# A gated linear attention kernel: scores and state updates as 64x64 products on quarters of the TensorE array

## The reference

```python
x = L0_attn_hidden_states                                 # (16, 512, 128)
q = relu(heads(norm(x) @ Wq)); k = relu(heads(norm(x) @ Wk)); v = heads(norm(x) @ Wv)
g = log_sigmoid(norm(x) @ Wg1 @ Wg2 + bg2) / 16           # one gate for each key feature
S_t = exp(g_t)[:, None] * S_{t-1} + k_t (outer) v_t       # a 64x64 state for each kv head
o_t = (q_t / 8) @ S_t
o = g_norm_weight * o * rsqrt(mean(o*o) + eps)            # per head
x = x + norm(o @ Wo)
x = x + norm(experts(norm(x)))                            # top 2 of 8, silu(x gate) * (x up), down
```

## Time and profile before

| what | value |
|---|---|
| time, median of 3 runs | 1351.63 us (1347.49 to 1352.96) |
| the profiled execution, its time | 1356.56 us |
| its span, first to last instruction | 1354.7 us |
| PE busy | 1251.3 us, 92% |
| DVE / ACT / POOL busy | 58% / 50% / 41% |
| one sequence in the middle of the loop | 55.2 us, PE busy 51.7 us |
| query phase of that sequence | 13.2 us, PE busy 10.6 us |
| expert tiles and sums | from about 925 us to the end |

### The profile page before, as it was taken

One profiled execution on the slowest core, in us unless ns is written; L12 is line 12 of the kernel. 1 busy time (PEld: TensorE's weight loads), 2 busy tenths in 40 slices (PEclk: granted clock), 3 DMA queues, 4 the chain that ended last, 5 costly groups with the idle time before them and its releaser, 6 DMA issues.

```text
span 1354.7 us, 27688 instructions
## 1 busy us (share of the span) xinstructions
PE 1251.3 (92%) x8062; PEld 1045.2 (77%) x8062; DVE 791.5 (58%) x2380; ACT 676.3 (50%) x1717; POOL 550.3 (41%) x671
## 2 busy tenths in 40 slices
PE   8999999989999899998998989956999999999895
PEld 5877868779687686786877868755989998998772
DVE  5676766667766676676766776662333333333327
ACT  4655547456464464654746547332444444444336
POOL 2244443544534435344363443332333333333326
PEclk9999999999998999999999999987999999999998
DMA  6000010100100001001010010132411111111335
GB/s 255 9 25 19 21 31 13 34 27 12 39 12 27 31 8 39 14 25 31 8 39 16 23 31 5 31 127 81 126 49 47 49 47 47 49 49 43 111 135 209
DMA packets 59674, 67.47 MB, mean 50 GB/s; under 512 B 6896, under 2 KB 49664, under 8 KB 59264
## 3 DMA queue, kind: packets, MB, share of 16 engines
q1 hardware_dynamic: 48720, 41.10, 9.6%
q0 software_dynamic: 8448, 17.45, 3.9%
q10 hardware_dynamic: 2480, 8.61, 2.0%
HBM read 37.98 MB, written 29.15 MB: 50 GB/s over the span
## 4 chain that ended last, share of the span: by engine, by line
PE 75%; DVE 10%; issue 6%; DMA 3%; ACT 3%; another core or an unknown queue 1%; POOL 1%; DVEq 1%; ACTq 0%; POOLq 0%; SPq 0%
PE pO L756 8%; PE pA L579 8%; PE pO L595 8%; PE pO L597 6%; PE pA L561 5%; PE pW L624 4%; PE pA L747 4%; PE pA L748 4%; PE pJ L747 4%; PE pJ L748 4%; PE pO L569 4%; PE pJ L561 3%; PE pT L607 3%; DVE kT L1103 2%; PE pJ L624 2%
## 5 line engine op out<-in xcount | busy, mean ns | idle before, releaser
L1591 POOL DMA_INDIRECT expert_out<-y,tail x136 | 130.5, 960 | 262.5 <-ACT y L1024 235.3
L595 PE MATMUL pO<-vJ,aT 128*128 128x128 f32 x1024 | 194.0, 279 | 0.0
L873 ACT ACTIVATE sq<-pO 128x512 f32<-128x512 f32 x128 | 75.9, 593 | 213.3 <-PE pO L595 170.4
L597 PE MATMUL pO<-S_mid,qT 128*128 128x128 f32 x896 | 173.2, 275 | 0.0
L595 PEld LDWEIGHTS pO<-vJ,aT 128*128 128x128 f32 x1024 | 153.8, 192 | 14.7 <-issue 13.2
L569 PEld LDWEIGHTS pO<-vJ,kJ 128*128 128x128 f32 x448 | 68.4, 200 | 102.6 <-issue 52.4
L1151 DVE TENSOR_REDUCE ss<-sq 128x8 f32<-128x512 f32 x128 | 86.6, 676 | 100.7 <-ACT sq L873 100.7
L1523 POOL DMA_INDIRECT expert_rows<-x1n,rowi x120 | 117.5, 979 | 65.0 <-issue 43.6
L597 PEld LDWEIGHTS pO<-S_mid,qT 128*128 128x128 f32 x896 | 136.0, 192 | 0.0
L579 PE MATMUL pA<-qT,kT 128*128 128x256 f32 x512 | 132.8, 383 | 0.0
L756 PE MATMUL pO<-wdown_sb,vJ 128*128 128x128 f32 x1088 | 132.7, 275 | 0.0
(11 more groups left out here) (239 smaller groups left out, 2602.3 us busy)
## 6 DMA issues: line engine op xcount, KB each, us to landing
xt<-expert_rows SPq DMA_DIRECT2D x69, 130.0 KB
xa<-x SPq DMA_DIRECT2D x16, 256.0 KB, 2.7
xr<-x SPq DMA_DIRECT2D x16, 256.0 KB, 2.8
after_attention<-x SPq DMA_DIRECT2D x16, 256.0 KB
arena<-after_attention ACTq DMA_DIRECT2D x8, 512.0 KB
expert_rows<-zeros SPq DMA_DIRECT2D x8, 390.0 KB
expert_out<-y,tail POOLq DMA_INDIRECT x136
wgate_sb<-wgate SPq DMA_DIRECT2D x1, 2048.0 KB, 9.9
```

Source lines behind the costliest of these rows:

```text
L595: last = mm(o, aT[:, c % 2, p, h * P:(h + 1) * P], vJ[:, c, p, :], start=True, stop=(c == 0))
L597: last = mm(o, qT[:, p, c, 2 * h:2 * h + 2, :].rearrange("p r c -> p (r c)"), S_mid[:, c, p, :], start=False, stop=True)
L1591: g.indirect_dma_start(out=ys_dram, in_=y[:, k, :], in_offset=None, out_offset=bass.IndirectOffsetOnAxis(ap=tail[:, k, 1:2].bitcast(U32), ...
```

## The change

Keys are stored compactly: `kT` holds 64 columns for each pair and chunk and has no zeros, `kJ` one 128x128 block a chunk. Scores are computed by 64x64 products: four for a chunk, one for each head, on the four quarters of the array (rows by head `h`, output partitions by pair `p`). They are issued for two chunks at a time, behind one semaphore increment. State updates are four 64x64 products of 64 columns a chunk, all 28 of them behind the second query. `S_raw` is 64 wide; `mids` on POOL spreads it back over two blocks with a mask of the halves (`own_step`). `outputs` does its four products of masked scores first and then the four with the state. DVE computes `kT` with two instructions on 128 partitions, the keys are seven transposes, and ACT copies them with two instructions.

```diff
-            def key_transposes(j, groups):
-                for p in range(PAIRS):
-                    pe.wait_ge(k_ready, j * 4 + 2 * p + 2)
...
-                        for c in range(2 * g, min(2 * g + 2, NC - 1)):
-                            last = tr(key_bank[g][:, ((c % 2) * 2 + p) * P:((c % 2) * 2 + p + 1) * P],
-                                      kT[:, p, c, :], ident)
+            def key_transposes(j):
+                pe.wait_ge(k_ready, j * 2 + 2)
+                for c in range(NC - 1):
+                    last = tr(key_bank[c // 4][:, c % 4 * P:(c % 4 + 1) * P],
+                              kT[:, c, :, :].rearrange("p a c -> p (a c)"), ident)
...
+            def project_queries(j, turns=range(PAIRS * R)):
+                for b in turns:
+                    if b < 2:
+                        pe.wait_ge(v_ready, j * 8 + 4 * b + 4)
+                    elif b < 4:
+                        pe.wait_ge(k_ready, j * 2 + b - 1)
+                    else:
+                        pe.wait_ge(q_ready, j * 8 + b - 3)
+                    mm(four[b % 4][:], wq_sb[:, b // R, b % R, :], xnT[:],
+                       start=True, stop=True).then_inc(q_psum, 1)
+                    if b == 1:
+                        state_updates(j)
+
+            def state_updates(j):
+                pe.wait_ge(kJ_ready, j * 2 + 2)
+                settle(pe)
+                for c in range(NC - 1):
+                    for p in range(PAIRS):
+                        for h in range(2):
+                            rows = slice(p * C, p * C + C)
+                            last = mm(pR[h * D:(h + 1) * D, p, c * D:(c + 1) * D], kJ[rows, c, h * D:(h + 1) * D],
+                                      vJ[rows, c, h, p * D:(p + 1) * D], start=True, stop=True)
+                last.then_inc(upd_psum, 1)
...
                 if c >= 2:
-                    pe.wait_ge(a_ready, i * NC + c - 1)
-                for p in range(PAIRS):
-                    if c < 2:
-
-                        pe.wait_ge(q_ready, i * 8 + (8 if p == 1 else 5 + c))
-                    last = mm(pA[c % 2][:, p, :], kT[:, p, c, :],
-                              qT[:, p, c, :, :].rearrange("p r c -> p (r c)"), start=True, stop=True)
+                    pe.wait_ge(a_ready, i * NC + c)
+                else:
+                    pe.wait_ge(q_ready, i * 8 + 8)
+                settle(pe)
+                for n in (c, c + 1):
+                    for p in range(PAIRS):
+                        for h in range(2):
+                            rows = slice(h * D, h * D + D)
+                            last = mm(pS[p * C:(p + 1) * C, h, n % 2 * R * C:(n % 2 + 1) * R * C], kT[rows, n, p, :],
+                                      qT[rows, p, n, :, :].rearrange("p r c -> p (r c)"), start=True, stop=True)
                 last.then_inc(a_psum, 1)
...
-                    if c + 2 < NC:
+                    if c % 2 == 0 and c + 2 < NC:
                         scores(i, c + 2)
...
-                    for half in range(2):
-                        rows = slice(half * D, half * D + D)
-                        v.scalar_tensor_tensor(
-                            out=kT[rows, p, :, half * C:half * C + C],
+                    v.scalar_tensor_tensor(
+                        out=kT[:, :, p, :], in0=pJ[p][:].rearrange("p (n c) -> p n c", c=C), scalar=0.0,
...
-                            scalar=step[:, p, c - 1:c], in1=pO[c % 2][:, p, :], op0=ALU.mult, op1=ALU.add)
+                            scalar=step[:, p, c - 1:c], in1=came[:, p, :], op0=ALU.mult, op1=ALU.add)
...
+                g.tensor_tensor(own_step[:, :, 0:NC - 1, :], wide(step[:, :, 0:NC - 1].unsqueeze(3), P, PAIRS, NC - 1, 2),
+                                wide(own_half.unsqueeze(1).unsqueeze(1), P, PAIRS, NC - 1, 2), ALU.mult)\
+                    .then_inc(own_ready, 1)
...
-                    g.tensor_tensor(S_mid[:, c + 1, :, :], S_raw[:, c % 2, :, :],
-                                    wide(step[:, :, c:c + 1], P, PAIRS, P), ALU.mult).then_inc(mid_ready, 1)
+                    g.tensor_tensor(S_mid[:, c + 1, :, :].rearrange("p a (h v) -> p a h v", h=2),
+                                    wide(S_raw[:, c % 2, :, :].unsqueeze(2), P, PAIRS, 2, D),
+                                    wide(own_step[:, :, c, :].unsqueeze(3), P, PAIRS, 2, D), ALU.mult)\
+                        .then_inc(mid_ready, 1)
```

More of the change, by code:

```diff
@@ L61 @@
 C_RB = C_RW + E
-C_LEAST = C_RB + E
+C_HALF = C_RB + E
+C_LEAST = C_HALF + 2
 C_END = C_LEAST + E
@@ L534, in project_values @@
                     last.then_inc(v_psum, 1)
-            def key_transposes(j, groups):
-                for p in range(PAIRS):
-                    pe.wait_ge(k_ready, j * 4 + 2 * p + 2)
-                    for g in groups:
-                        if p == 0 and g < 3 and not at_start(j):
-                            pe.wait_ge(*((on_ready, j * NC), (on_ready, j * NC), (ot_ready, j * NC))[g])
-                        for c in range(2 * g, min(2 * g + 2, NC - 1)):
-                            last = tr(key_bank[g][:, ((c % 2) * 2 + p) * P:((c % 2) * 2 + p + 1) * P],
-                                      kT[:, p, c, :], ident)
-                        if p == PAIRS - 1:
-                            last.then_inc(kJ_psum, 1)
@@ L591, in outputs @@
                     pe.wait_ge(mid_ready, i * (NC - 1) + c)
+                o = pO[c % 2][:].rearrange("t (p g) (h v) -> t g h p v", p=PAIRS, h=2)
+                for h in range(2):
+                    for g in range(2):
+                        last = mm(o[:, g, h, :, :], aT[:, c % 2, h, g * P:(g + 1) * P], vJ[:, c, h, :],
+                                  start=(h == 0 and g == 0), stop=(c == 0), skip_group_check=True)
                 for p in range(PAIRS):
-                    for h in range(2):
-                        o = pO[c % 2][:, 2 * p + h, :]
-                        last = mm(o, aT[:, c % 2, p, h * P:(h + 1) * P], vJ[:, c, p, :], start=True, stop=(c == 0))
+                    for g in range(2):
                         if c > 0:
-                            last = mm(o, qT[:, p, c, 2 * h:2 * h + 2, :].rearrange("p r c -> p (r c)"),
-                                      S_mid[:, c, p, :], start=False, stop=True)
+                            last = mm(pO[c % 2][:, 2 * p + g, :],
+                                      qT[:, p, c, 2 * g:2 * g + 2, :].rearrange("p r c -> p (r c)"),
+                                      S_mid[:, c, p, :], start=False, stop=True, skip_group_check=True)
                 last.then_inc(o_psum, 1)
@@ L630, in chunks @@
                 scores(i, 0)
-                scores(i, 1)
                 for c in range(NC):
@@ L706, in turn @@
                 project_values(i + 1)
-                key_transposes(i + 1, range(NC // 2))
+                key_transposes(i + 1)
                 merge_heads(i, NT - 1, True)
-                project_queries_and_states(i + 1)
+                project_queries(i + 1)
             turn(0, False)
@@ L857, in values @@
                         came = slice(odd * C, odd * C + C)
[L858 to L861 removed]
+                        for p in range(PAIRS):
+                            goes = slice(p * C, p * C + C)
+                            a(tiles[goes, :, odd, :, p * D:p * D + D],
+                              pA[g][came, :, :].rearrange("p t (q h d) -> p t q h d", h=2, d=D)[:, :, p, :, :],
                               ACT.Copy).then_inc(v_ready, 1)
             def keys(j):
[L865 to L868 removed]
+                for g in range(2):
+                    act.wait_ge(kJ_psum, j * 2 + g + 1)
+                    n = UPTO[g] - 4 * g
+                    a(kJ[:, 4 * g:4 * g + n, :].rearrange("p c j -> p (c j)"), key_bank[g][:, 0:n * P],
                       ACT.Copy).then_inc(kJ_ready, 1)
```

92 lines of the change are left out of this document (35 added, 57 removed).

## The result

The changed kernel took 1384.28 us (median of 4 runs, 1383.15 to 1386.08), the kernel before beside it 1350.31 (4 runs, 1347.49 to 1352.96): a ratio of 1.0253, 95% interval 1.0232 to 1.0275. It is slower by 34 us, where 32 us less had been forecast. The profiled execution took 1384.46, its span is 1382.7.

The account below looks back on a forecast made before the run. PE was taken to bound the chunk phase, an order of waits the query phase. −1.9 us in 16 chunk phases and −0.1 in 15 query phases gave −32: 1320 us against 1351.6, range 1290 to 1390.

Parts of the forecast that it names:

- State updates: Query phase, 28 64x64 products on PE: cost nothing, up to 2 us without cover; DVE's states gain 0.6 to 0.7.
- the keys: Before the queries: two DVE instructions for four save 1.5 us; third query 1.0 us earlier, bounds 0 and 1.5.
- the chunk phase: PE-bound stretch of 31.50 us: three more score groups −2.6, six width changes +0.7, together −1.9 us in each of 16.
- The clock: PE idles 3.1 us before first scores; half clock follows in six of ten sequences: +0.9 us, bounds −0.4 and +2.8.
- G: PE time of one group of scores products for two chunks: 1.0 us, quarters running at once; 1.74 before.
- First outputs behind the last query: End of query phase: a whole scores group now stands behind the last query, 2.2 us instead of 1.62, +0.6.
- Changes of the width: Chunk phase: six changes between 128- and 64-wide products at 0.12 us each, +0.7; range 0 to 1.6.
- DVE's pace of a query and a state: Query phase: a state's two DVE instructions take 0.06 us less each at 64 columns instead of 128.
- Pairs in line: Rival: each product's two instructions run strictly in order, so groups take 1.95 us and gain nothing; 1375 us, chance 0.30.
- Serial quarters: Rival on the scores products: the array's quarters do not overlap, a group takes 3.6 us; 1484 us, chance 0.07.
- rule on draining: Chunk phase: changing tiling mode drains TensorE; by it width changes cost 1.6 us, not 0.7, total 14 us worse.
- the clock falls in every sequence: Rival: full overlap, but half clock after the idle stretch in all 15 query phases, +2.8 for +0.9; 1348 us, chance 0.08.

Follow-up runs that it names:

- halves kernel: Changed kernel with each chunk's state update as two 128x64 products instead of four 64x64, still in one block behind the second query: 1353.88 us, ratio 1.0007.
- v1: The halves kernel with every state update computed twice, in the same block behind the second query: 1388.65 us, ratio 1.0269.
- spread kernel: The halves kernel with updates spread, one chunk behind each query from the second on: 1315.25 us, ratio 0.971; repeats 1306.17 and 1314.14 us.
- v2: Changed kernel with 14 blank bf16 products ahead of the first scores: 1372.79 us, ratio 1.0152.
- x7: The spread kernel with 12 blank bf16 products behind the sixth query: 1297.98 us on one chip (ratio 0.9887), 1305.28 us on another (0.963).
- x3: Kernel before, with 56 tiny full-array bf16 products of no use behind the first chunk's state update: 1419.33 us, ratio 1.0489.
- x5: The spread kernel with every state update computed twice: 1305.52 us on one chip (ratio 0.9944), 1355.42 us on another (1.0012).

## Why the prediction was wrong

**The step that failed** is "State updates", in "cost nothing, and if that cover were gone, up to 2 us". The 28 products were priced by array time and by weight loads, 0.8 to 3.1 us, and the first 40 records of them (0.81 us) bear that out. What was left out is that they are twice as many instructions, all moved ahead of the scatter's end. The block took 7.4 us (465.64 to 473.01) instead of 1, and from the queries to the scores 4.7 us a sequence were lost, a part of it to the clock. Beside the scatter PE ran some 67 records (64 to 72) before it stopped. By the scatter's end the changed kernel wants 7 + 16 + 4 + 56 = 83 and the four queries (8) behind them, the halves kernel 63 with them. The cover that hid them, DVE's late third query, was there. But it is itself made by the scatter, and PE was held by the same. The working had seen that scatter and DVE hinder each other and that the rows did not say by what. It then treated the hindrance as DVE's alone, and as a cover that the change could rely on.

The kernels give the parts in total time. All the rest of the change, with 28 products of 128x64 for the updates, spread: 1314 against 1353, −39. These moved into one block: +38 (1352, halves), of which the rows show DVE's hold and PE idle behind it (2.91 us). Twice their number: +34 (1386 to 1389, changed kernel and v1). The forecast of −32 is the time of the spread kernel: 53.2 us a sequence by its terms, 53.20 in the trace.

The sequence agrees to the hundredth by luck: the query phase of the spread kernel is not the one forecast (PE waits 1.93 us for a state in it, and 0.25 ahead of the scores), and its three sets lie at −37, −44 and −39 us. What the agreement supports is the keys and the chunk phase.

**The clock** went the forecast's way but too little: +0.9 a sequence, from six sequences in ten. In the changed kernel each of the 14 sequences with a trickle runs 6.8 us at 1.2 GHz, from within the trickle on (at 470 in the sequence shown), and 3.4 us more from about the first outputs on. The second is 1.6 us each (v2 and the spread kernel), near the 1.7 that had been worked out. The first was not in the forecast, since its wait was not. The idle stretch of 3.1 us ahead of the first scores was 1.24: DVE was no longer four queries behind.

**Right:** the keys, 1.5 forecast, 1.6 measured. G, 1.0 forecast: a group starts at 479.95 and the outputs behind it at 480.98, 1.03. First outputs behind the last query, 2.2 forecast: 483.57 − 481.44 = 2.13. Changes of the width, 0.12 each: eight outputs ahead of a group take 1.08 (478.87 to 479.95) instead of 0.99 in the earlier trace rows, 0.09. DVE's pace of a query and a state: 1.12 in the earlier trace rows, 0.99 now (one begins at 477.81, the next at 478.80), 0.13 less where 0.12 was forecast. The chunk phase: −1.9 forecast, 29.38 − 27.75 = −1.6 at full clock.

**The rivals.** Pairs in line would have made G 1.95; it is 1.03, so this rival, which had 0.30 and a time near the measured one (1375), was wrong in mechanism. The Trainium skill (TensorE: Matmul & The Clock Gate, Part 3) has products start and end in program order; here that order cost no overlap between the quarters, although each product is two instructions. Serial quarters: refuted by the same row. The Trainium skill's rule on draining (TensorEngine Tiling (Array Packing), Key Properties) goes with a price of 0.09 us for a change to the quarters, so by the rows it was no argument against this change. That the clock falls in every sequence was right as far as it went. The true cause was in none of the rivals.

**Left open:** what keeps the instructions from coming. The rows show idle time without a cause, a limit of about 67 records (64 to 72) in three kernels of different make, and an end of the trickle 1.5 us behind the last scatter instruction. The Trainium skill (Advanced Engine Details and Errata, ISA Cache) says that an engine keeps its instructions in a few cached blocks of 256; no run here shows the blocks. Their loading would be the next guess, but the changed kernel's trace speaks against it: its DMA queues of the kind "instruction" moved 27 packets on the page, and none between 125 and 890 us, where 13 of the 14 trickles lie. All queues that moved anything in that window:

```profile
q1 hardware_dynamic: 21264, 10.62, 4.9%
q0 software_dynamic: 3328, 6.93, 2.8%
```

Also open is what differs on the quick chip: its DVE is not held and its PE not bound to 67 records (rows above), but the changed kernel was not run there.

## What to carry to other kernels

Count instructions, not only array time, between the start and the end of a stretch of indirect transfers set off by GpSimd: two small products cost as many as two large ones, and a block that takes 1 us alone took 7.4 beside the scatter. Where such a stretch can't be moved without making its queue late, spread the work over it in the order in which the waiting engine will take it. Where a wait remains ahead of a full stretch, a few blank products in it were worth 0.6 to 0.9 us a sequence here (v2 and x7); there they stood behind the end of the transfers. Blanks beside them (x3) cost time.

## What the hardware showed that was not expected

Four quarters of the array run products of 64x256 float32 at once: 16 records in 1.03 us, where full-array products for the same scores took 1.74. Beside eight indirect transfers (9.95 us) TensorE ran 64 to 72 records and then only a few each 0.7 to 1.5 us, in three kernels and 14 sequences of each, while the traced queues loaded no instructions (125 to 890 us). VectorE was held for 2.2 to 5.1 us in the same time, with its input ready. And chips differ in it: the kernel before took 1350 to 1354 us on four chips and 1312.9 on a fifth at the same mean clock (0.98), where VectorE was not held in the spread kernels (x5 and x7) and TensorE once ran 80 records beside the transfers.
